# Attention 0's queries as Strassen's seven products of halves, with the operand sets formed in the prologue and fetched from DRAM a block ahead

## What is computed

```
q = (query @ wq).reshape(b, tq, HQ, D)        # HQ 32, D 128, 512 features in
k = (key @ wk).reshape(b, tk, HKV, D)         # HKV 8
v = (value @ wv).reshape(b, tk, HKV, D)
scores = jnp.einsum('bqhd,bkhd->bhqk', q * D ** -0.5, repeat(k, 4))
probs = jax.nn.softmax(scores, axis=-1)
out = jnp.einsum('bhqk,bkhd->bqhd', probs, repeat(v, 4)).reshape(b, tq, HQ * D)
return out @ wo
```

## Time and profile before

| | us |
|---|---|
| median of 3 runs | 1642.33 |
| lowest, highest | 1639.29, 1645.27 |
| the profiled execution's own time | 1639.45 |
| its span | 1637.7 |
| attention loop, one trip of four blocks | 116.8 |
| first query product starts at | 56.3 |
| granted TensorE clock, mean | 0.974 |

### The profile page before, as it was taken

The page is one execution under the profiler, slowest core; times in us unless marked ns, Lnnn a source line. Parts: engine busy times, 40 slices in busy tenths (PEclk is TensorE's granted clock), DMA queues, the critical chain, the costliest instruction groups (busy, mean ns, idle before and its releaser), DMA issues. The chain is left out here.

```text
span 1637.7 us, 29866 instructions
## 1 busy us (share of the span) xinstructions
PE 1493.0 (91%) x11323; PEld 795.2 (49%) x11323; DVE 1250.3 (76%) x2330; ACT 831.1 (51%) x1757; POOL 267.8 (16%) x245
## 2 busy tenths in 40 slices
PE   5799999999999999999999986799999987787695
PEld 4455555555555555555555542344445544343353
DVE  6577667668677667767776786799999985999777
ACT  3433434424334243343333332888989864888652
POOL 2001002001011011011011000001111103889620
PEclk9899999999999999999999998899999999999898
DMA  7022231322313222221321123122223250867402
GB/s 270 1 78 52 67 90 27 79 77 44 100 39 59 85 58 59 65 65 53 78 52 53 37 93 117 24 46 46 45 47 64 59 97 1 149 107 121 78 1 103
DMA packets 274122, 114.06 MB, mean 70 GB/s; under 512 B 239184, under 2 KB 255696, under 8 KB 273744
## 3 DMA queue, kind: packets, MB, share of 16 engines
q1 hardware_dynamic: 235104, 79.26, 23.1%
q10 hardware_dynamic: 38896, 33.03, 6.3%
HBM read 45.15 MB, written 11.53 MB: 35 GB/s over the span
## 5 line engine op out<-in xcount | busy, mean ns | idle before, releaser
L583 PE MATMUL pj<-XT,WQ 128*128 128x512 f16 x1536 | 338.5, 380 | 6.4 <-PEq L377 6.4
L625 PE MATMUL xp<-WO,OT 128*128 128x512 f16 x1536 | 340.9, 382 | 3.7 <-DVE X L822 3.7
L625 PEld LDWEIGHTS xp<-WO,OT 128*128 128x128 f16 x1536 | 148.2, 98 | 187.5 <-issue 16.5
L583 PEld LDWEIGHTS pj<-XT,WQ 128*128 128x128 f16 x1536 | 148.5, 98 | 181.6 <-DVE WKV L292 6.6
L822 DVE SCALAR_TENSOR_TENSOR X<-xp,X 128x512 f32<-128x512 f32 x128 | 88.2, 690 | 114.9 <-PE xp L625 114.9
L1027 PE MATMUL db<-W0T,XD 128*128 128x448 f16 x768 | 152.2, 359 | 23.2 <-DVE XD L1226 23.2
L707 ACT ACTIVATE E<-E 128x512 f32<-128x512 f32 x64 | 40.1, 627 | 262.3 <-DVE E L799 262.3
L563 POOL TENSOR_TENSOR VW<-VW,XB 128x1024 f32<-128x1024 f32 x14 | 33.0, 2358 | 757.7 <-DVE VW L105 757.7
L1042 PE MATMUL eb<-W1T,DT 128*128 128x512 f16 x672 | 147.7, 379 | 4.1 <-DMA DT<-HL 2.2
L764 DVE SCALAR_TENSOR_TENSOR QT<-pj,QT 128x512 f16<-128x512 f32 x128 | 87.8, 686 | 55.4 <-ACT QT L686 55.4
L1027 PEld LDWEIGHTS db<-W0T,XD 128*128 128x128 f16 x768 | 75.8, 99 | 98.2 <-DVE XD L1226 23.7
(11 more groups left out here) (228 smaller groups left out, 2397.2 us busy)
## 6 DMA issues: line engine op xcount, KB each, us to landing
W0T<-in_L_xattn_wq ACTq DMA_DIRECT2D x7, 1024.0 KB, 5.2
W0T<-in_L_xattn_wo ACTq DMA_DIRECT2D x7, 1024.0 KB, 5.1
CS<-in_ctx SPq DMA_DIRECT2D x4, 1024.0 KB, 10.1
X<-in_x SPq DMA_DIRECT2D x4, 1024.0 KB, 11.2
out<-X SPq DMA_DIRECT2D x8, 512.0 KB, 3.6
XB<-in_L_ffn_W ACTq DMA_DIRECT2D x28, 128.0 KB, 2.7
w0t<-XB ACTq DMA_DIRECT2D x7, 512.0 KB, 3.3
w1t<-W0T ACTq DMA_DIRECT2D x7, 512.0 KB, 3.8
```

Source lines behind the costliest of these rows:

```text
L583: last = pe.matmul(bank[:, :], w, src[:, b, k, tokens], start=n == 0, stop=n == 3 * KC - 1)
L625: last = pe.matmul(xp[i % 2][:, :], OT[:, a, j, i * P:(i + 1) * P], WO[:, b, j, :], start=n == 0, stop=n == 3 * REP - 1)
```

## The change

The query projection of a block, 512 tokens by 512 features by 512 columns (4 heads), is split into halves of each size and formed as seven products of 256 by 256 by 256 (Strassen's scheme in the form with 15 additions, four on each side and seven on the result) in place of eight.

- The seven operands from `x` (four quarters and sums, XR) are made in the prologue. GpSimd forms the four sums (TX) from the normalised tiles, TensorE transposes seven units in place of four, ScalarE and VectorE split them, and SP stores each block's set, 1.84 MB, to a DRAM tensor (xsets). XT is gone. In attention, SP fetches a block's set one block ahead into the one buffer XR, in two pieces (products 0 to 4, and 5 and 6), behind the transposes of the probabilities.
- The seven operands from `wq` are made per group: ScalarE scales SQ in place at the end of t = 1, GpSimd forms four sums, at the end of t = 2 ScalarE writes the high parts in three steps, VectorE the low parts of three operands and GpSimd that of the four sums.
- A product is 12 matmuls of 256 columns into one bank; 84 in a block, where 48 of 512 stood. Products 0 to 4 come first, then keys and values, pair 0, products 5 and 6, pair 1. In the last group's t = 2 products 5 and 6 come ahead of pair 0 and the values behind it (`early`).
- Products are added up outside PSUM: ScalarE copies product 0 to QA, VectorE makes five sums (add_query) into QA's three buffers, two products are added in the bank itself. One quarter of the queries is split from the bank by ScalarE and VectorE, the other three from QA, by ScalarE (high) and GpSimd (low). Products 2, 4, 5 and 6 use the output projection's banks xp, so the projection waits for the last two sums, and product 2 for the last accumulation into X.
- The prologue's semaphores are cleared as before; those of attention 0 are now cleared in the next stage.

The core of the diff:

```diff
+SETS = 7
+HALF = BLOCK // 2
+Q_WEIGHTS = (A11, S2, S1, A12, S3, A22, S4)
...
+        def scale_q(act, g):
+            act.wait_ge(W["sq_ld"], g * 16 + 16)
+            act.activation(SQ[:, :, :], SQ[:, :, :], ACT.Copy, scale=WEIGHT_SCALE).then_inc(W["qkv_hi"], 1)
+
+        def sum_q(pool, g):
+            pool.wait_ge(W["qkv_hi"], g * 5 + 1)
+            pool.tensor_tensor(TW[:, 0], weight_block(1, 0), weight_block(1, 1), ALU.add).then_inc(W["q_sums"], 1)
+            pool.tensor_tensor(TW[:, 2], weight_block(0, 0), weight_block(1, 0), ALU.subtract).then_inc(W["q_sums"], 1)
...
...
         def high_q(act, g):
-            act.activation(WQ[:, 0, :, :], SQ[:, :, :], ACT.Copy, scale=WEIGHT_SCALE).then_inc(W["qkv_hi"], 1)
+            act.wait_ge(W["q_sums"], g * 4 + 4)
+            to, source = first_columns(0)
+            act.activation(to, source, ACT.Copy).then_inc(W["qkv_hi"], 1)
...
+            act.activation(WQ[:, 0, S1:, :, :], TW[:, :, :, :], ACT.Copy).then_inc(W["qkv_hi"], 1)
...
+        def low_q_sums(pool, g):
+            pool.wait_ge(W["qkv_hi"], g * 5 + 4)
+            pool.tensor_tensor(WQ[:, 1, S1:, :, :], TW[:, :, :, :], WQ[:, 0, S1:, :, :], ALU.subtract).then_inc(W["qs_lo"], 1)
...
+                for i in range(BLOCKS):
+                    sp.wait_ge(lo_done, unit_end(i, PER - 1))
+                    sp.dma_start(set_rows(i, 0, SETS), staged[i].rearrange("p s h c n -> p (s h c n)")).then_inc(W[f"xset_st{i}"], 16)
+                    if i == 2:
+                        sp.wait_ge(W["xset_st2"], 16)
+                        load_o(sp, 0)
...
+                    pool.wait_ge(xn_ready, blk * BT + BT)
+                    if blk:
+                        pool.wait_ge(tp_done, unit_end(blk - 1, PER - 1))
+                    near_x, far_x = whole_tiles(0), whole_tiles(1)
+                    left, right = slice(0, HALF), slice(HALF, DIM)
+                    pool.tensor_tensor(TX[:, 0], far_x[:, :, left], near_x[:, :, left], ALU.subtract).then_inc(tx_ready, 1)
+                    pool.tensor_tensor(TX[:, 1], far_x[:, :, right], far_x[:, :, left], ALU.subtract).then_inc(tx_ready, 1)
+                    pool.wait_ge(tx_ready, blk * 4 + 1)
+                    pool.tensor_tensor(TX[:, 2], far_x[:, :, right], TX[:, 0], ALU.subtract).then_inc(tx_ready, 1)
+                    pool.wait_ge(tx_ready, blk * 4 + 3)
+                    pool.tensor_tensor(TX[:, 3], near_x[:, :, right], TX[:, 2], ALU.subtract).then_inc(tx_ready, 1)
+                    if blk == 2:
+                        sum_q(pool, 0)
+                low_q_sums(pool, 0)
...
+                    if g < GROUPS - 1 or t < SPG - 2:
+                        sp.wait_ge(S["pt_done"], n_of(g, t, 32, 32))
+                        for lo, hi in ((0, 5), (5, SETS)):
+                            sp.wait_ge(S["qp_done"], n_of(g, t + 1, SETS, hi))
+                            load_sets((t + 2) % SPG, lo, hi)
...
+            def low_queries(g, t):
+                for n in range(3):
+                    pool.wait_ge(S["q_hi"], n_of(g, t, 4, n + 2))
+                    i, j, buffer = ((1, 1, 1), (1, 0, 0), (0, 1, 2))[n]
+                    pool.tensor_tensor(queries(1, i, j), query_sum(buffer), queries(0, i, j), ALU.subtract).then_inc(S["q_lo"], 1)
...
+            def query_products(g, t, which):
+
+                first = isinstance(g, int) and g == 0 and t == 0
+                for n in which:
+                    if n == 0:
+                        pe.wait_ge(S["qkv_lo"], g * 3 + 3)
+                        pe.wait_ge(S["qs_lo"], g + 1)
+                        if not first:
+                            pe.wait_ge(S["xr_ld"], n_of(g, t, 32, 0))
+                            pe.wait_ge(S["kv_lo"], n_of(g, t, 2, 0))
+                    elif n == 2 and not first:
+                        pe.wait_ge(S["x_acc"], n_of(g, t, 4, 1 - 4))
+                    elif n == 3:
+                        pe.wait_ge(S["q_first"], n_of(g, t, 1, 1))
+                    elif n == 5:
+                        pe.wait_ge(S["q_add"], n_of(g, t, 5, 2))
+                    elif n == 6:
+                        pe.wait_ge(S["q_add"], n_of(g, t, 5, 3))
+                    fresh = n in (0, 1, 2, 4)
+                    for m in range(2):
+                        for step, (c, (a, b)) in enumerate([(c, ab) for ab in PASSES for c in range(2)]):
+                            last = pe.matmul(head_columns(Q_BANKS[n], m), WQ[:, a, Q_WEIGHTS[n], c, m * P:(m + 1) * P],
+                                             XR[:, n, b, c, :].rearrange("p (b t) -> p b t", b=4), start=fresh and m == 0 and step == 0, stop=step == 5, skip_group_check=True)
+                    last.then_inc(S["qp_done"], 1)
...
+                    early = last and t == SPG - 2
                     if more:
-                        project(*nxt, range(4))
-                    if more:
-                        project(*nxt, (4,))
+                        query_products(*nxt, range(5))
+                        project_keys(*nxt)
+                        if early:
+                            query_products(*nxt, (5, 6))
+                        else:
+                            project_values(*nxt)
                     weigh_values(g, t, 0)
                     if more:
-                        project(*nxt, (5,))
+                        if early:
+                            project_values(*nxt)
+                        else:
+                            query_products(*nxt, (5, 6))
                     weigh_values(g, t, 1)
-                    if last and t == SPG - 2:
+                    if early:
                         scores(g, SPG - 1)
-                    project_out(g, t)
+                    project_out(g, t, more)
...
+            def first_query(g, t):
+                act.wait_ge(S["qp_done"], n_of(g, t, SETS, 1))
+                act.activation(QA[:, 0, :], pj[0][:, :], ACT.Copy, scale=UNSCALE).then_inc(S["q_first"], 1)
+
+            def high_query(g, t, n):
+                if n == 0:
+                    act.wait_ge(S["qp_done"], n_of(g, t, SETS, 4))
+                    act.activation(queries(0, 0, 0), query_bank(pj[0]), ACT.Copy, scale=UNSCALE).then_inc(S["q_hi"], 1)
+                else:
+                    act.wait_ge(S["q_add"], n_of(g, t, 5, n + 2))
+                    i, j, buffer = ((1, 1, 1), (1, 0, 0), (0, 1, 2))[n - 1]
+                    act.activation(queries(0, i, j), query_sum(buffer), ACT.Copy).then_inc(S["q_hi"], 1)
...
+                    early = last and t == SPG - 2
                     if more:
-                        high(*nxt, range(2, 4))
+                        high_query(*nxt, 1)
                     for p in prepared(t, last):
                         weights_times_rec(g, *p)
                     if last and t in (1, 2):
...
-                        high(*nxt, (4,))
+                        high_keys(*nxt)
+                        if early:
+                            high_query(*nxt, 2)
+                            high_query(*nxt, 3)
+                        else:
+                            high_values(*nxt)
                     high_out(g, t, 0)
                     if more:
-                        high(*nxt, (5,))
+                        if early:
+                            high_values(*nxt)
+                        else:
+                            high_query(*nxt, 2)
+                            high_query(*nxt, 3)
                     high_out(g, t, 1)
+                    if t == 1 and not last:
+                        scale_q(act, g + 1)
...
+            def add_query(g, t, n):
+
+                done, bank, other, to = ((2, pj[1], 0, 2), (5, xp[0], 2, 1), (3, xp[1], 1, 1), (6, xp[0], 2, 0), (7, xp[1], 2, 2))[n]
+                dve.wait_ge(S["qp_done"], n_of(g, t, SETS, done))
+                if n == 0:
+                    dve.wait_ge(S["q_first"], n_of(g, t, 1, 1))
                 else:
+                    dve.wait_ge(S["q_add"], n_of(g, t, 5, 2 if n == 2 else 1))
+                dve.scalar_tensor_tensor(out=QA[:, to, :], in0=bank[:, :], scalar=UNSCALE, in1=QA[:, other, :],
+                                         op0=ALU.mult, op1=ALU.add).then_inc(S["q_add"], 1)
...
+                    early = last and t == SPG - 2
+                    if more:
+                        add_query(*nxt, 0)
                     for jp in range(2):
                         sums(g, t, jp)
-                        if more:
-                            low(*nxt, jp)
                         normalise(g, t, jp)
                     low_probs(g, t, 0)
+                    if more:
+                        low_query(*nxt)
                     low_probs(g, t, 1)
                     if more:
-                        low(*nxt, 2)
+                        add_query(*nxt, 1)
                     if t == 0:
                         dve.wait_ge(S["o_hi"], g + 1)
```

(15 more changed lines are left out.)

339 lines of the change are left out of this document (224 added, 115 removed).

## The result

| kernel | median, us | runs | ratio to before, 95% interval |
|---|---|---|---|
| before | 1641.95 | 4 (1639.29 to 1645.27) | 1 |
| changed | 1718.19 | 4 (1715.58 to 1724.27) | 1.0469 (1.0434 to 1.0503) |

The direction was forecast, the size was not: 76 us more where 22 were forecast, and the time lies outside the range of 1640 to 1680.

What follows compares the result with a forecast made beforehand. The prediction took TensorE, busy 91% overall and throughout the loop, to bound the kernel. Prologue 13.5, first block 3.6, loop 0 and last group 4.7 sum to +21.8 on 1642.3, so 1664 us, range 1640 to 1680.

Steps and rivals of the forecast that it cites:

- Matmul time: Query products: 84 matmuls of 256 columns at 109.3 ns replace 48 of 512, gaining 1.18 us a block, 33.0 in the loop.
- Stalls at weigh 1 and PT: Attention loop: TensorE waits for VectorE's low output and the transposed probabilities, 2.6 + 0.4 + 1.15 + 0.55 = 4.7 us a group.
- The loop comes out even: Attention loop: 4.7 us of stalls a group against 4.7 of gain, net 0; bounds minus 16 and plus 9 us.
- GpSimd's subtractions run beside VectorE ... 0.3 for each overlap, not on the chain above: Attention loop: a VectorE operation beside GpSimd takes 0.98 us against 0.68, so 0.3 an overlap, off the critical chain.
- the query sums themselves would be done in time: End of t = 2: GpSimd's group sums end at about +27.3 us, with product 0 due at 29.
- Rival 2, the clock: TensorE's clock falls in the pauses at t = 0, 1.7 us for each of 7, giving 1676 us; chance 0.13.
- Rival 1: Loop: shorter chain, TensorE stays full, all 33.0 us gained, 1631 us; decided by ScalarE's copy before 9.6; chance 0.15.
- Rivals 3 and 4: 256-column matmuls cost 127 ns, 1685 us, chance 0.06; the operand-set fetch is late, 1720 us, chance 0.03.
- Prologue: Up to the first product: more evictions, GpSimd's sums and the weights' sums add 13.5 us (11 to 16).
- First block: First attention block: scores' waits, a later fetch and the clock, less the matmul gain, add 3.6 us (1 to 6).
- Last group: Last attention group: the next norm's moments, later table load and two more adds add 4.7 us (2 to 7).

Runs made afterwards that it cites:

- e4: The changed kernel with ScalarE's four weight loads in t = 0 moved from ahead of the key copy to behind the value copy; 1698.02 us.
- e1: The changed kernel with 80 waits on an already set semaphore (40 instructions) first in TensorE's queue, moving only its code's place; 1687.17 us.
- e2: The kernel before with 362 such idle waits (181 instructions), so its loop starts where the changed kernel's does; 1669.9 us.
- e3: The changed kernel with GpSimd's 2048-element subtraction for the weight sums' low part left out of the loop (8 elements instead); 1698.8 us.
- e5: The changed kernel with VectorE's steps of t = 2 reordered: L105 ahead of the low query weights, L107 and L110 behind the third accumulation; 1716.45 us.
- e6: The changed kernel with GpSimd's 2048-element subtraction cut into four of 512, VectorE's order untouched; 1707.81 us.
- e8: The changed kernel with e1, e4 and e5 together and several more ScalarE and VectorE steps moved, same arithmetic; 1650.56 us.
- e11: e8 plus e9's exchange, the last group's norm maxima and scales one accumulation later in t = 1, and GpSimd's loop subtraction cut in four; 1639.22 us.
- e7: The changed kernel with GpSimd's four sums of each prologue block cut to copies of 8 columns; 1714.6 us.
- e9: e5 plus ScalarE forming the high keys-and-values weights ahead of the sums', VectorE their low part right behind the low query weights; 1716.67 us.

## Why the prediction was wrong, point by point

The step that failed is the loop. Its working set 4.7 us of waits a group against 4.7 of gain and called it even; the gain and these waits came as forecast, and 46.7 us stood beside them for which it had no term (18.5 + 8.7 idle, 19.5 of half clock and the rest).

- **Matmul time** (33.0 gained in the loop): right, 1.18 us a block. The products are 109 ns a matmul apart.
- **Stalls at weigh 1 and PT** (4.7 a group, 33): right in place and near in size, 36.3. In nearly all groups t = 0 had 1.9 to 2.6 of the forecast 2.6, besides 0.6 to 0.8 for PT that was not forecast there; t = 1 0.43 of 0.4; t = 2 0.47 + 0.31 of 1.15; t = 3 1.1 of 0.55. e4 shows the cause of the largest.
- **"The loop comes out even"**, with bounds of minus 16 and plus 9: wrong, plus 48.9. Three terms were missing. The branch back (18.5 idle): the working took a trip to be as long as its matmuls and waits, and never asked where the longer code ahead of the loop would put the loop's code. e1 and e2 settle it for the second pause (14.1); what makes the first (4.4) longer than before the change stays open. The waits for the first product copy and for the accumulation (8.7 idle): see the next point. The half clock behind the pauses (about 15, with the rest 19.5).
- **"GpSimd's subtractions run beside VectorE ... 0.3 for each overlap, not on the chain above"**: this step failed too. The price came from an overlap in the earlier trace rows that happened to be short: L811 started at 488.08, and GpSimd's operation beside it ended at 488.52. A held step waits for all that is left of GpSimd's operation, which made L107 3.3 us longer here, and at the end of t = 2 that is on the chain. e3, e5 and e6 show it. That the query sums themselves would be done in time was right (at +26.8 of t = 2, for +27.3). The section of the Trainium skill that the prediction cited beside it names the same contention without a size; that "the sum would be the same by either" was wrong.
- **Rival 2, the clock** (0.13, +12): its mechanism was there together with the forecast, not in its place. The pauses at t = 0 of 1.9 to 2.6 us, those at the branch of 2.2 to 2.7 and the rest cost about 15 us in the loop. Without the pauses at the branch (e1) TensorE's busy time is 6.8 us less, without those at t = 0 (e4) 5.4 less; e8 to e11 have hardly any of it left.
- **Rival 1**, the other side, named its condition wrong: a copy before 9.6 at t = 0 alone would not have done. e11, in which the other waits are gone too or shorter, still has a loop of 798, not of 783.
- **Rivals 3 and 4** did not come: 256 columns at 109 ns, and no product waited for XR. That the 1720 of rival 4 lies next to the measured 1718 is chance.
- **Prologue** +15.5 of 13.5, in its bounds; the split between GpSimd and evictions was put too far on GpSimd's side (e7). **First block** +1.4 of 3.6, in its bounds: scores waited 2.67 us for GpSimd's low queries as laid out, the rest was too dear.
- **Last group** +7.2 of 4.7 (its terms, minus 1.2, 3.5 and 2.3, add up to 4.6), just over its bound. The three waits in it:

```profile
1005.52 1.46 PE L793 MATMUL tv<-PT,V 64*128 64x256 f16 x12 [4.68 <-DVE OT L1011]
...
1034.61 2.74 PE L749 MATMUL xp<-XR,WQ 128*128 128x256 f16 x12 [3.91 <-DVE QA L990]
...
1045.44 0.83 PE L793 MATMUL tv<-PT,V 64*128 64x256 f16 x12 [3.05 <-DVE OT L1011]
```

The middle one was not forecast: in t = 2 products 5 and 6 come early and use the bank that add 2 must leave, and add 2 stood behind the norm's moments.

- **The range.** Its ends were sums of known terms. Every new kind of wait could only add, and none was allowed for.

## What to carry to other kernels

A loop that is full to the last matmul has no room for a new pause: each one costs its length, some cost half clock behind it as well, and together they were more than the whole gain. When a change lengthens the code ahead of a loop, look at the first instructions behind the branch in the trace, and try the loop's place by itself with some idle instructions in front; it cost 22 us of the loop here and had nothing to do with the idea. When work goes to GpSimd, list which VectorE steps run beside it and keep to SBUF (here the cuts and the steps with two SBUF inputs; the reductions were not held), charge each the rest of GpSimd's operation, and put steps that read PSUM there, or cut the operation short.

## What the runs showed of the hardware

- TensorE stood for 2.0 to 2.7 us at each branch back when 27 instructions of a 16 KB packet were left at the loop's start, and not when 208 or 243 were. The pause right behind the branch was 0 to 0.6 us in the kernel before, 0.4 to 1.1 in the changed one and 0.6 to 1.8 in e1, e8 and e11.
- 181 instructions that wait on a set semaphore, ahead of TensorE's first work, put its first matmul at 20.67 us in e2 (6.42 before) and the first product 8.1 us later, while 40 delayed neither in e1 (6.42 against 6.55, 71.10 against 71.79).
- A GpSimd operation held VectorE steps of 0.68 and 1.22 us for 3.96, 4.56 and 4.50 us (the cuts L107 and L105, and L334 with two SBUF inputs), and left an accumulation with a PSUM input and a reduction with one SBUF input at 0.68.
- For the same matmuls TensorE's busy time in the loop was 786.5 us in e11, 801.8 in the changed kernel and 811.8 in e9: the granted clock stood at 1.00, 0.98 and 0.97.
